# The order of the second layer's products in a mixture-of-experts kernel: by tile instead of by half of the hidden layer

## The reference, cut to what matters

```python
def _L0_ffn_ref(x, router_w, w_gate, w_up, w_down):      # x: 4096 rows of 256, after a layernorm
    routing = jax.nn.softmax(xf @ router_w.T, axis=-1)    # 8 experts
    top_w, top_i = lax.top_k(routing, 2)                  # 2 experts for each row
    ...
    g = jnp.einsum('nd,ehd->neh', xf, w_gate)             # 256 -> 512
    u = jnp.einsum('nd,ehd->neh', xf, w_up)
    h = jax.nn.silu(g) * u
    y = jnp.einsum('neh,edh->ned', h, w_down)             # 512 -> 256, "the second layer"
    out = jnp.einsum('ned,ne->nd', y, combine)
x = x + tanh(g_xattn) * attention(layernorm(x), ctx)      # ahead of it, in the kernel's first part
x = x + tanh(g_ffn) * _L0_ffn_ref(layernorm(x), ...)
```

## Time and profile before

| | us |
|---|---|
| median of 3 runs | 441.66 (437.33 to 444.09) |
| the profiled execution: its time | 438.52 |
| the profiled execution: its span, first to last instruction | 436.7 |
| PE busy in the span | 413.7 |
| DVE busy | 314.8 |
| ACT busy | 285.4 |
| POOL busy | 251.4 |

### The profile page before, as it was taken

How to read it: one execution, slowest core, us unless ns; L and a number is a source line. 1 busy time by engine, 2 the same in 40 slices (tenths; PEclk the granted TensorE clock), 3 DMA queues, 4 the chain that set the end, 5 groups by cost and what they waited for, 6 DMA issues and landing times.

```text
span 436.7 us, 9843 instructions
## 1 busy us (share of the span) xinstructions
PE 413.7 (95%) x3237; PEld 378.9 (87%) x3237; DVE 314.8 (72%) x707; ACT 285.4 (65%) x581; POOL 251.4 (58%) x271
## 2 busy tenths in 40 slices
PE   8999889967899999999999999999999999999991
PEld 3778665534799999999999999999999999999991
DVE  4448999994476777767767777777776777777771
ACT  2698786302377767677676776767767677676770
POOL 5015446434236665766676665676667676567664
PEclk9999999988799999999999999999999999999997
DMA  6956866777457775434333343333433334333343
GB/s 196 328 181 210 267 211 207 248 245 235 109 141 162 162 162 138 67 59 69 50 56 57 59 72 49 54 58 60 66 55 53 56 61 68 55 52 58 63 64 65
DMA packets 34720, 50.52 MB, mean 116 GB/s; under 512 B 3878, under 2 KB 26055, under 8 KB 34695
## 3 DMA queue, kind: packets, MB, share of 16 engines
q0 software_dynamic: 13536, 19.46, 27.2%
q1 hardware_dynamic: 19815, 29.84, 22.2%
q10 hardware_dynamic: 1344, 0.92, 0.7%
HBM read 32.51 MB, written 17.70 MB: 115 GB/s over the span
## 4 chain that ended last, share of the span: by engine, by line
PE 75%; DVE 7%; DMA 7%; ACT 4%; issue 3%; POOL 2%; ACTq 1%; POOLq 0%; DVEq 0%
PE GT L1182 21%; PE Y L1203 20%; PE UP L1182 20%; DMA out_rows<-y,idx 4%; PE W L1030 3%; PE XT L1173 3%; DMA brow<-in_b_row 2%; DVE at_low L801 2%; PE O L1105 2%; ACT ex L582 2%; PE S L1055 2%; POOL xt L495 1%; DVE at_tile L949 1%; ACTq L538 1%; DMA xt<-xn_rows,idx 1%
## 5 line engine op out<-in xcount | busy, mean ns | idle before, releaser
L503 POOL DMA_INDIRECT out_rows<-y,idx x68 | 114.3, 1681 | 97.3 <-ACT y L654 66.6
L973 DVE TENSOR_TENSOR gu<-raw,gu 128x1024 fp32r<-128x1024 f32 x70 | 85.8, 1226 | 65.1 <-ACT gu L630 62.3
L1182 PE MATMUL GT<-xtT,gu 128*128 128x256 f32 x828 | 114.5, 288 | 2.6 <-DVE xtT L973 1.4
L495 POOL DMA_INDIRECT xt<-xn_rows,idx x76 | 97.1, 1277 | 33.7 <-issue 22.9
L1182 PE MATMUL UP<-xtT,gu 128*128 128x256 f32 x828 | 111.2, 284 | 0.0
L1182 PEld LDWEIGHTS GT<-xtT,gu 128*128 128x128 f32 x828 | 104.7, 193 | 4.6 <-DVE xtT L973 1.8
L1182 PEld LDWEIGHTS UP<-xtT,gu 128*128 128x128 f32 x828 | 105.0, 193 | 0.0
L1203 PE MATMUL Y<-dn,hT 128*128 128x256 f32 x816 | 103.5, 283 | 0.0
L1203 PEld LDWEIGHTS Y<-dn,hT 128*128 128x128 f32 x816 | 100.4, 192 | 0.0
L630 ACT CAST gu<-raw 128x1024 fp32r x68 | 70.8, 1042 | 34.3 <-PE UP L1182 31.9
L994 DVE TENSOR_TENSOR hid<-hid,UP 128x512 f32<-128x512 f32 x68 | 46.5, 684 | 9.3 <-PE UP L1182 9.0
(11 more groups left out here) (156 smaller groups left out, 382.5 us busy)
## 6 DMA issues: line engine op xcount, KB each, us to landing
raw<-in_weights SPq DMA_DIRECT2D x32, 384.0 KB
xn_rows<-pay SPq DMA_DIRECT2D x8, 528.0 KB, 3.6
xTg<-in_xT SPq DMA_DIRECT2D x8, 512.0 KB, 4.2
xg<-in_x SPq DMA_DIRECT2D x8, 512.0 KB, 6.0
out_rows<-xg SPq DMA_DIRECT2D x8, 512.0 KB, 3.0
xt<-xn_rows,idx POOLq DMA_INDIRECT x76
out_rows<-y,idx POOLq DMA_INDIRECT x68
kr<-in_ctx_rows SPq DMA_DIRECT2D x1, 308.0 KB
```

The lines of the kernel that those rows point to most:

```text
L495: gp.indirect_dma_start(out=xt[:, 2 * s + t, :], out_offset=None, in_=xn_rows, in_offset=bass.IndirectOffsetOnAxis(ap=idx[:, 2 * j + t:2 * ...
L503: gp.indirect_dma_start(out=out, out_offset=bass.IndirectOffsetOnAxis(ap=idx[:, 2 * j + t:2 * j + t + 1], axis=0), in_=y[:, j % 2, t, :], ...
L973: return tt(out=out, in0=whole, in1=high.bitcast(F32), op=ALU.subtract)
L1182: last = mm(bank[:, h * PT:(h + 1) * PT], gu[:, pw, q, c, w, h * P:(h + 1) * P], xtT[:, b, px, c], start=(c == 0 and n == 0), stop=(c == D ...
```

## The change

In `down` the loop over the tiles t becomes the outer one and the loop over the halves q the inner one. Before, the order of the 24 products was: 6 of half 0 for tile 0, 6 of half 0 for tile 1, 6 of half 1 for tile 0, 6 of half 1 for tile 1. After, it is: 6 of half 0 and 6 of half 1 for tile 0, then the same for tile 1. The waits for `hid_low` stand ahead of the first product of each half, and `down_ready` is raised behind the last product of each tile, in both. No product is added or left out, and the sum in each bank is made in the same order.

```diff
             def down(j, b):
                 pe.wait_ge(dn_low, j + 1)
                 pe.wait_ge(y_ready, 2 * j + Y_READY0)
-                for q in range(2):
-                    pe.wait_ge(hid_low, 2 * j + q + 1 + LOW0)
-                    for t in range(2):
+                for t in range(2):
+                    for q in range(2):
+                        if t == 0:
+                            pe.wait_ge(hid_low, 2 * j + q + 1 + LOW0)
                         for c in range(2):
                             for px, pw in HI_LO:
                                 last = mm(Y[:, t, 0:D], hT[:, px, 2 * q + c, t * P:(t + 1) * P],
                                           dn[:, pw, b, q, c * D:(c + 1) * D],
                                           start=(q == 0 and c == 0 and px == 0 and pw == 0),
                                           stop=(q == 1 and c == 1 and px == 1))
-                        if q == 1:
-                            last.then_inc(down_ready, 1)
+                    last.then_inc(down_ready, 1)
```

## The result

| | before | after |
|---|---|---|
| median of 6 runs, us | 437.69 (435.44 to 444.09) | 444.98 (440.33 to 449.40) |
| ratio | | 1.0116 (95% interval 1.0063 to 1.0169) |
| span of the profiled execution, us | 436.7 | 443.3 |
| first load of the first `down` to first load of the last | 300.85 | 305.76 |

With three more runs the median of before went down by 4 us. The medians are over all six runs of each kernel, and the ratio leaves out the runs that fell in the chip's slower state (two of the kernel after, 448.26 and 449.40), so the ratio is the number to read.

The account below looks back on a forecast made before the run. PE was taken to bound the expert part; stops of 5.75 us, less 0.13 and 0.20 at the end, gave 5.4 us, 1.2%: 443.9 us against the profiled execution, 447.1 on the median, range 442 to 452.

Parts of the forecast that it names:

- PE bounds the expert part and a stop isn't won back: In the expert part the chain is PE alone, without slack, so 0.1 us of stop in each of 34 turns is 3.4 us.
- The data of the second half end 0.79 to 0.80 us after the first load, product 7 allows 0.72: In `down` with s = 1 to 3, DVE's `hT` subtraction ends after product 7's load is due; 0.93 us with s = 0.
- The signal costs 0.05 us, not 0.23: PE's load in `down` starts 0.05 us after DVE's data end; 0.23, seen in a wait for ACT, was kept as upper end.
- Rival A: Each stop in `down` costs 0.23 us of signal instead of 0.05: 11.5 us more, 453 us; chance 0.11 including uncovered loads.
- Its variant with the uncovered loads: Loads uncovered after each stop in `down` add 3.4 us: 8.8 us in all, 450.5 us; included in the chance of 0.11.
- A stop costs 0.13 and 0.26 us: Ahead of product 7 of `down`: 0.13 us in 25 turns, 0.26 in 8 with s = 0, 0.42 in pair 32; 5.75 us.
- the restart after the stop: In `down`, the first product follows its load by 0.11 us as in steady flow, so nothing is added; upper end 3.4 us.
- The end of the kernel: The last `down`'s 0.13 us stop is hidden and 0.20 us of pair 32's delay taken up, leaving 5.4 us.
- The earlier `down_ready` brings nothing because ACT comes to y from its own queue: Tile 0's signal comes 0.72 us earlier, less the stop, for 0 us gain; at most 0.7 at the end if ACT were free.
- Rival B: No stop in `down`, and the early signal shortens the kernel's end by up to 0.7 us: 441.0 us; chance 0.07.
- Rival C: Stops lower the granted clock; a turn at 0.50 would be about 7 us longer, two such exceed 2%; chance 0.02.
- What the profile after would show: Y loads split 6 and 18, 0.01 to 0.15 us idle; `down` 9.20 us apart with s = 1 to 3; clock 1.00.

Follow-up runs that it names:

- E4: Kernel before, products in old order, with the wait for the second half of `hT` moved ahead of product 1 of `down`: ratio 1.0682 to the kernel before.
- E1: Kernel before, products and `down_ready` in old order, with only the wait for the second half of `hT` moved ahead of product 7: ratio 1.0118 to the kernel before.
- E5: Kernel before, products in old order, with the wait for the second half of `hT` moved ahead of product 9: ratio 1.0021 to the kernel before.
- E6: Changed kernel, with y of tile 0 written ahead of the cast of `dn` on ACT: ratio 1.0098 to the kernel before.
- E2: Changed kernel, with the second half of `hT` made ahead of the rows of pair j+2 on ACT and DVE: ratio 1.0052 to the kernel before.
- E8: Kernel before, with only ACT's read of pair j's expert number moved behind the casts at the head of a turn: ratio 0.9964 to the kernel before.
- E7: Changed kernel with the edits of E2 and E6, and pair j's expert number read later on ACT: 434.89 us, ratio 0.9954 to the kernel before.
- E3: Kernel before, with only E2's exchange on ACT and DVE: ratio 0.9981 to the kernel before.

## Why the prediction was right

- *PE bounds the expert part and a stop isn't won back.* Right. E4 is the proof: 28.9 us of stops in the 33 turns that its stretch counts. For these 33 the expectation is 25 x 0.84 + 7 x 0.97 + 1.14 = 28.9 us.
- *The data of the second half end 0.79 to 0.80 us after the first load, product 7 allows 0.72.* Right, and unchanged after the change (298.52 - 297.73 = 0.79). With s = 0 and in pair 32 it was right too (0.90 to 0.93 and 1.10). E1 shows that the wait's place is the whole cause; E4, E1 and E5 give the scale: ahead of product 1, 7 and 9 the stretch grows by 28.9, 4.95 and 0.46 us.
- *The signal costs 0.05 us, not 0.23.* Right: 0.05 in E4's chain. Rival A falls; it had the distance at 9.35 us and it is 9.18. Its variant with the uncovered loads, 8.8 us in all, falls by the 4.9 us of the stretch.
- *A stop costs 0.13 and 0.26 us.* Right for load 7, a little too much for what follows. The 24 products take 2.99 instead of 2.88 us and 3.12 in the turn with s = 0, so 0.11 and 0.24. The term that was mis-sized is the restart after the stop. I added nothing for the uncovered load and kept up to 0.10 us more as the bad end; it is 0.02 us the other way, some 0.7 us over all turns. Load 7 is 0.13 us late, but the four steps from load 7 to load 11 take 0.46 instead of 0.48 us in the turn shown, and y of tile 1 is late by 0.11. What lets them stand closer isn't shown. By the Trainium skill's rule for a load ("TensorE: Matmul & The Clock Gate", section "Part 2: What happens when you issue a matmul") an estimated 3.6 us should have come on top; no run here shows such a term.
- *The end of the kernel.* Wrong in one step. I took 0.20 us off because the add before had landed at 426.15, 0.20 us after the y of tile 0 had ended, and read that landing as what the add of tile 0 waited for. But this add starts 1.04 to 1.05 us after the end of its own y in all ten executions, and anything from 0.56 to 1.78 us after that landing. So it hangs on y, and the delay goes through in full: the last `down` came 4.94 us later than before, and this add too (431.94 - 427.00). Without the 0.20 the sum is 5.6 us.
- *The sum.* 5.4 us were forecast. The stretch grew by 4.9 and the last `down` has another 0.11, which the end hides. The two errors, 0.7 us too much in the restart and 0.2 too little at the end, have opposite signs. In the profiled execution the whole is 6.6 us, through one late landing that no step foresaw. In the ratio it is 1.16% against 1.2% forecast, but with an interval of 0.63 to 1.69% that closeness says little; it is the stretch that tests the sum. That the measured median, 444.98 us, lies near the forecast 447.1 is luck in part: the forecast hung on a median of three runs that lay 4 us above that of six, and from the median of six it would have been 442.9.
- *The earlier `down_ready` brings nothing because ACT comes to y from its own queue.* Right: y of tile 0 at 2.70 us, as before. E6 measures what it hid: 0.67 us, once, at the end of the kernel, against the 0.7 us at most of the prediction.
- *Rival B* (no stop) falls by the trace after. E2 makes its condition true for three turns of four, and the stop is gone there. The Trainium skill's "Loop structure matters more than you think" (in "TensorE: Matmul & The Clock Gate") shows one output tile with all its K tiles as the good form. It sets it against a loop that waits for a DMA ahead of every product, not against two tiles by turns. Here that form is neither good nor bad by itself: with the same place of the wait both orders cost the same, and what counts is how much of the work ahead needs no fresh data.
- *Rival C* (the clock): 1.00 in the expert part, even in E4.
- *What the profile after would show.* The split into 6 and 18 loads appears only where the stop is 0.24 us; the stops of 0.11 us are inside one group of 24, which is 3.06 us long instead of 2.95. The prediction expected the split everywhere, with at most 0.15 us idle; with s = 0 it is 0.19. The distance of two `down` is 9.18 us where 9.20 was expected. It expected y of tile 1 with the same 0.18 us of idle time, and this was a slip: tile 0 is served as early as before and the 24th product is 0.11 us later, so it had to grow, to 0.29.

## What to carry to other kernels

When a loop nest is turned round, ask for each operand that is still being made how many products stand ahead of its first use, and compare their time with the moment it is ready: here the time of six products was 0.07 us too short (0.13 with the signal), and every turn paid. A signal that comes earlier is worth something only if the engine that takes it is free; otherwise put its work earlier in that engine's queue too, or leave it. And where one engine is busy all the time, look for the places where its pace breaks at the head of a loop: reading one register later gave 0.36% (0.04 to 0.67%), more than the 0.15% that the earlier signal of tile 0 could give at most.

## What the runs showed that I had not expected

- The turn with s = 0 doesn't follow the chain of the others. After the exchange in E2 its stop stayed at 0.24 us (load 7 at 377.56, first load at 376.58), since it begins with ACT's reads of the expert numbers. With one of them later the subtraction ended at 0.79 instead of 0.93 us (E8), and together with the exchange (E7) both that stop and the 0.17 us ahead of the gate were gone in the turn shown.
- The last add of 128 rows starts 0.27 us after the one before it has landed, in all ten executions, and the distance between the two was 4.02 to 5.73 us. That is a scatter of 1.7 us at the end of a kernel whose whole effect was 5 us.
- Single gathers land late, in some executions and not in others. The transposes stopped for one of them by 0.24 us in E5, 0.44 in E3 and 0.17 in E8, and not in the turns of before. So a difference of some 0.5 us between two stretches can be one gather.
